# A decoder layer in fp32 on one core: a twelfth half of the product by C is computed on the vector engine, the second half of tile 12

## The reference, cut to what matters

```python
dA = exp(delta[l, d] * A[d, n])              # (L, 512, 16)
dBu = delta[l, d] * B[l, n] * u[l, d]
carry = dA * carry + dBu                     # restarts every 64 tokens
y[l, d] = sum over n of carry[l, d, n] * C[l, n]
y = y * silu(res);  y @ W_out.T + b_out
```

## Time and profile before

| | us |
|---|---|
| median of 3 runs (lowest, highest) | 2745.58 (2741.46, 2746.72) |
| the profiled execution | 2741.8 |
| its span in the profile | 2740.0 |
| POOL, DVE, ACT, PE busy in the span | 2073.6, 2123.5, 1821.1, 2429.5 |

### The profile page before, as it was taken

The page is one execution under the profiler, slowest core; times in us unless marked ns, Lnnn a source line. Parts: engine busy times, 40 slices in busy tenths (PEclk is TensorE's granted clock), DMA queues, the critical chain, the costliest instruction groups (busy, mean ns, idle before and its releaser), DMA issues. The chain is left out here.

```text
span 2740.0 us, 49530 instructions
## 1 busy us (share of the span) xinstructions
PE 2429.5 (89%) x14854; PEld 1667.0 (61%) x14854; DVE 2123.5 (77%) x3232; ACT 1821.1 (66%) x3972; POOL 2073.6 (76%) x999
## 2 busy tenths in 40 slices
PE   6678898989898898889999989988997879999997
PEld 5456666666666666666666666666665545555554
DVE  3788999999999999999999999999999722222333
ACT  3667888888888888888888887888887531111111
POOL 5999999999999999999999999999999400000000
PEclk9888999999999999999999999999998869999999
DMA  5355666666666666666666666666665342432221
GB/s 154 112 152 147 168 168 161 160 167 170 175 161 168 171 171 163 163 165 167 165 165 176 160 177 162 171 163 160 160 160 156 101 118 65 119 120 80 80 80 31
DMA packets 270168, 399.66 MB, mean 146 GB/s; under 512 B 115441, under 2 KB 190449, under 8 KB 265810
## 3 DMA queue, kind: packets, MB, share of 16 engines
q1 hardware_dynamic: 254546, 384.95, 52.9%
q10 hardware_dynamic: 15360, 11.55, 1.6%
HBM read 300.89 MB, written 94.37 MB: 144 GB/s over the span
## 5 line engine op out<-in xcount | busy, mean ns | idle before, releaser
L519 POOL TENSOR_TENSOR arena<-arena 128x1024 f32<-128x1024 f32 x512 | 1207.6, 2364 | 33.6 <-DMA arena<-w_dram 33.3
L623 ACT ACTIVATE dA_ps<-arena,a_neg 128x256 f32<-128x256 f32 x2048 | 880.1, 465 | 256.3 <-DVE arena L800 125.7
L800 DVE TENSOR_TENSOR_SCAN arena<-dA_ps,arena 128x512 f32<-128x512 f32 x672 | 802.7, 1207 | 75.5 <-ACT dA_ps L623 52.2
L529 POOL TENSOR_TENSOR arena<-arena 128x1024 f32<-128x1024 f32 (+1 forms) x416 | 808.4, 1943 | 18.0 <-DVE arena L800 15.0
L800 DVE TENSOR_TENSOR_SCAN dA_ps<-dA_ps,arena 128x512 f32<-128x512 f32 x352 | 415.7, 1204 | 3.8 <-POOL arena L519 3.4
L920 PE MATMUL a_ps<-xT,w_conv 128*128 128x256 f32 x1536 | 367.3, 389 | 0.0
L863 DVE TENSOR_REDUCE mx<-s_ps 128x2 f32<-128x512 f32 x497 | 333.4, 671 | 18.6 <-PE s_ps L920 18.6
L920 PEld LDWEIGHTS a_ps<-xT,w_conv 128*128 128x128 f32 x1536 | 286.5, 193 | 53.9 <-issue 16.3
L679 ACT ACTIVATE probs<-st_ps 128x512 f32<-128x512 f32 x493 | 285.2, 578 | 27.6 <-PE st_ps L920 25.4
L920 PE MATMUL s_ps<-k_st,q_st 96*128 96x256 f32 x994 | 262.2, 346 | 38.8 <-DVE mx L863 29.3
L920 PE MATMUL y_ps<-arena,sel 128*32 128x256 f32 x4096 | 258.5, 395 | 37.5 <-POOL arena L529 33.9
(11 more groups left out here) (117 smaller groups left out, 3275.4 us busy)
## 6 DMA issues: line engine op xcount, KB each, us to landing
arena<-delta_dram SPq DMA_DIRECT2D x512, 128.0 KB, 2.9
arena<-w_dram SPq DMA_DIRECT2D x512, 128.0 KB, 3.3
arena<-bc_dram SPq DMA_DIRECT2D x128, 256.0 KB, 4.5
q_st<-q_parts_dram SPq DMA_DIRECT2D x512, 64.0 KB
k_st<-k_parts_dram SPq DMA_DIRECT2D x512, 64.0 KB
w_dram<-u SPq DMA_DIRECT2D x32, 512.0 KB, 3.1
delta_dram<-delta SPq DMA_DIRECT2D x32, 512.0 KB, 3.9
k_parts_dram<-parts SPq DMA_DIRECT2D x32, 512.0 KB, 4.2
```

Of the source, the lines that this page charges most:

```text
L519: pool.tensor_tensor(dBu[:, n % NB], w_r[:, n // RP % 2, t % RP].unsqueeze(1).to_broadcast([P, QS, L]), bc_r[:, b.par, 0], ALU.mult).then_ ...
L529: pool.tensor_tensor(h[:, n % NH, states], h[:, n % NH, states], bc_r[:, b.par, 1, states], ALU.mult).then_inc(s_hC, 1)
L623: last = nc.scalar.activation(dA[n % NDA][:, q], delta_r[:, n // (2 * RP) % 2, t % RP], ACT.Exp, scale=a_neg[:, t, 2 * half + q:2 * half + ...
L800: nc.vector.tensor_tensor_scan(dst, decays, dBu[:, n % NB, 2 * half:2 * half + 2].rearrange("p q t -> p (q t)"), 0.0, ALU.mult, ALU.add).t ...
```

## The change

One entry, (12, 1), joins the list. DVE's scan of half 1 of tile 12 now writes to its PSUM bank, and a new L813 follows it; POOL's L529 for tile 12 shrinks from 1024 to 512 elements and waits for the scan of half 0 instead of half 1. ACT's decay of half (14, 0), which reuses that bank, waits for the new L813. The counts in the other waits follow the list's length.

```diff
-HC_DVE = [(1, 0), (1, 1), (4, 1), (5, 0), (5, 1), (6, 1), (8, 0), (9, 1), (10, 0), (10, 1), (14, 1)]
+HC_DVE = [(1, 0), (1, 1), (4, 1), (5, 0), (5, 1), (6, 1), (8, 0), (9, 1), (10, 0), (10, 1), (12, 1), (14, 1)]
```

## The result

The changed kernel takes 2771.56 us (median of 4 runs, 2768.8 to 2775.79) against 2746.15 us for the kernel before, measured beside it: a ratio of 1.0104, 95% interval 1.009 to 1.0118, so 25 us slower. The forecast was 2755.5 us, with a range up to 2768. The direction was right; the forecast was short by 16 us, and the result lies above the range.

A forecast was written before the change was run, and what follows sets the result against it. It took one DVE-PE-DVE chain per quiet period, not POOL, as the bound. Steady periods +11.4 us, last batch +0.7 and start -2.2 gave +9.9 us, put on the median 2745.58: 2755.5 us, range 2745 to 2768.

The forecast's parts named there:

- The floor of a period: Quiet period, L507 to next L507, 65.3 us: the L813 in DVE's stretch without a wait adds 0.72 us.
- POOL's relief: Between L507 and the next batch's first dBu: POOL's saved 1.09 us becomes waiting for the w load, gain 0.
- The start: First two batches, where POOL waits for almost nothing: the saved 1.09 us comes off twice, -2.2 us.
- The sum over the steady periods: 27 periods grouped by excess over the quiet floor, each group's share of the added 0.72 us summed: +11.4 us.
- the 13 periods: Periods with 0.69 to 1.92 us excess, PE or w load late behind tile 12: addition mostly hidden, 2.0 us taken.
- its 4 periods: Periods with 0.36 to 0.83 us excess arising in front of the new instruction: no later slack, 2.9 us in all.
- Rival 3: Addition costs in every batch and PE's clock falls more often: 22 us, 2768 us, chance 0.15.
- the 1.33 us wait at 634.49: PE waiting for DVE's L853 in a quiet batch: said to bring no clock fall, though as long as the lengthened wait.

The follow-up runs named there:

- pool_only: Kernel before with POOL's product for tile 12 cut to 512 elements, half 1 not multiplied by C anywhere: 2739.52 us, ratio 0.9993 to before.
- dve_only: Changed kernel with the lost 512 elements given back to POOL as a product nobody reads: 2769.93 us, ratio 1.0114 to the kernel before.
- after_fill: Changed kernel with matmuls repeated in PE's waits (scores head 11, scores_T heads 2 and 7, pv first group): 2743.0 us, ratio 1.0004 to before.
- after_fill_20: Changed kernel with only the scores_T of head 7 computed four times, before PE's wait at 18.5 us: 2753.04 us, ratio 1.0034 to before.
- no_14: Kernel before with (12, 1) on DVE's list in place of (14, 1), still 11 halves: 2761.95 us, ratio 1.0076 to before.
- place_7_1: Kernel before with half 1 of tile 7 added to DVE's list instead of tile 12's, 12 halves: 2749.93 us, ratio 1.0031 to before.
- thirteen: Kernel before with half 1 of tile 7 and half 1 of tile 12 both added, 13 halves: 2773.03 us, ratio 1.0124 to before.
- place_2_1: Kernel before with half 1 of tile 2 added to DVE's list instead of tile 12's, 12 halves: 2738.59 us, ratio 0.9994 to before.
- swap_4_2: Kernel before with half 1 of tile 2 on DVE's list in place of half 1 of tile 4, 11 halves: 2731.97 us, ratio 0.9962 to before.
- swap_4_23: Kernel before with half 1 of tiles 2 and 3 on DVE's list in place of half 1 of tile 4, 12 halves: 2720.66 us, ratio 0.9923.

## Why the prediction was wrong in size

- *The floor of a period, +0.72 us.* Right: 66.04 instead of 65.3, tile 12's pair 2.97 us, PE's wait 1.36, POOL's wait for the load longer.
- *POOL's relief, 0 in the steady part.* Right, and shown by pool_only and dve_only. The rule of the most-contended engine in the Trainium skill ("Perfetto Trace Analysis", "Identifying the Most-Contended Engine") names POOL here, as the engine to optimise first. This case does not bear it out: POOL's 97.7% was the highest share, and its relief gave a ratio of 0.9993 (0.9979 to 1.0006), no gain.
- *The start, -2.2 us.* Not borne out, and too small for these runs to decide. The fourth L507 came 0.66 us earlier, and in pool_only, with the same relief, 0.9 us later; but over the 17 profiled executions it lies anywhere from 283.5 to 290.5 us, with the relief or without. POOL does wait for ACT's delta there now (0.85 us at 91.22), where it had waited for nothing, so a part of the saving may have turned into a wait.
- *The sum over the steady periods, +11.4 us.* It fits the bare chain: with the stays filled away, +11.3 us, since there the mean excess over the floor fell from 0.45 to 0.12 us a period. The addition did fit under much of what is late anyway, as the prediction said of the 13 periods. That the single terms are right isn't shown, since the periods are made up otherwise in those kernels. The step that failed is what this sum leaves out: it takes the unevenness of the periods as given, and prices a change in PE's clock at nothing. The unevenness was to a large part clock already: all of its 4 periods have a stay at their start, and 9 of its 13 have one at 4.5 to 5.6 or at 18 to 21 us. Without the repeats the excess didn't shrink but grew, from 0.73 us a period to 0.99, and the steady part by 27.3 us instead of 11.4. The change brought 8 more periods with a stay near the 20th microsecond and 9 more with one at the start, worth 15.9 us.
- *Rival 3* named the lower clock, at a chance of 0.15. That its 2768 us came near the result is luck. It is 31 x 0.72 = 22 us and has no price for the clock in it; the bare cost was 13.7 us, and the stays made up the rest. It also looked at the wrong place: the wait that the change lengthens. I set against it that the 1.33 us wait at 634.49 "brings none in the quiet batch". That row was a quiet period's, chosen for being quiet; 2 of the 27 periods before already had a stay just there.

What stays open is why 10 periods had a stay behind the wait for L853 instead of 2, since that wait is 1.33 us in most periods of both kernels. The runs narrow it down. Such stays seem to need a long wait there: where it is 0.6 to 0.8 us (after_fill, after_fill_20, no_14) there were none, though the last two have the lengthened wait at 9.8 us. (One of the 10 in the kernel after has two shorter waits in its place, 0.46 and 0.74 us.) And the 1.33 us don't suffice: place_7_1 has them in 20 periods, with the short wait at 9.1 us, and no stay. The lengthened wait is not the whole cause either, since 6 stays were left where it was filled. What makes them frequent is something that comes with (12, 1): the profiled executions of after, dve_only and thirteen have 10, 12 and 10, those of before, pool_only, place_2_1, place_7_1, swap_4_2 and swap_4_23 have 2, 1, 0, 0, 1 and 1. It may be the length of the period itself, which no run separates from (12, 1): the shortest is 66.0 or 66.1 us in the first three and 65.3 or less in the other six. Nor did a run change the lengths of the two waits in fine steps.

## What to carry to other kernels

Read a period, not a share: find in one quiet period the chain of who waits for whom, and price the addition at its place in it; the same instruction cost 25 us at tile 12 and nothing at tile 2. Then ask where the excess over the quiet period comes from before letting anything be absorbed in it, and look at the granted clock in the long periods as well as in the quiet one. Where TensorE's short waits inside a loop bring stays at the lower clock, repeating a few matmuls in them is a cheap test of how much of the time is clock, and it can stay in the kernel if it gains.

## What was not expected of the hardware

- A wait of TensorE of 1.33 us, in front of a stretch in which it is busy throughout (20.02 of 20.20 us in the earlier trace rows), was followed by a stay at the lower clock in some periods and not in others with the same wait: 2 of 27 before, 10 of 27 after. One such stay made a period 1.45 us longer, one at the start of the period 0.65; both together gave 68.15 = 66.04 + 0.66 + 1.45.
- More work on TensorE made the kernel faster: 918 more matmuls, 28.5 us less between the kernel after and after_fill.
